# Where the two state-free matmuls stand in a ConvLSTM step

## The reference

```
def step(carry, xr):
    h, c = carry
    inp = jnp.concatenate([xr, h], axis=1)
    gates = lax.conv_general_dilated(inp, w_mid, (1,), 'SAME', ...) + b[None, :, None]
    i, f, g, o = jnp.split(gates, 4, axis=1)
    c2 = jax.nn.sigmoid(f) * c + jax.nn.sigmoid(i) * jnp.tanh(g)
    h2 = jax.nn.sigmoid(o) * jnp.tanh(c2)
    return ((h2, c2), h2)
```

## Time and profile before

| | |
|---|---|
| median of 3 runs | 1986.39 us (1983.12 to 1989.28) |
| the profiled execution's own time | 1985.13 us |
| its span | 1983.2 us |
| mean granted TensorE clock | 0.93 |
| PE busy | 1589.4 us (80%) in 13002 matmuls |
| DVE, ACT, POOL busy | 1475.4, 1172.0, 642.3 us |
| the two scans | about 275 to 798 us and 916 to 1443 us |

### The profile page before, as it was taken

One profiled execution on the slowest core, in us unless ns is written; L12 is line 12 of the kernel. 1 busy time (PEld: TensorE's weight loads), 2 busy tenths in 40 slices (PEclk: granted clock), 3 DMA queues, 4 the chain that ended last, 5 costly groups with the idle time before them and its releaser, 6 DMA issues. The chain is left out here.

```text
span 1983.2 us, 41167 instructions
## 1 busy us (share of the span) xinstructions
PE 1589.4 (80%) x13002; PEld 935.5 (47%) x13002; DVE 1475.4 (74%) x2699; ACT 1172.0 (59%) x2257; POOL 642.3 (32%) x577
## 2 busy tenths in 40 slices
PE   8979248888888888704888888888860899999997
PEld 6535125555555555203555555555520344445444
DVE  4539978888888888646888888888856766666666
ACT  1116128888888888543888888888853344444431
POOL 2010035555555555203555555555500000000000
PEclk9989669999999999857999999999985799999999
DMA  3769366666666666666666666667576011011100
GB/s 108 254 196 211 97 137 108 108 106 107 107 107 107 107 106 91 113 147 131 106 107 107 107 107 107 107 108 108 81 121 164 14 34 34 21 31 35 35 19 25
DMA packets 132266, 199.40 MB, mean 101 GB/s; under 512 B 28528, under 2 KB 47824, under 8 KB 131920
## 3 DMA queue, kind: packets, MB, share of 16 engines
q1 hardware_dynamic: 132176, 198.08, 53.7%
HBM read 73.72 MB, written 37.75 MB: 56 GB/s over the span
## 5 line engine op out<-in xcount | busy, mean ns | idle before, releaser
L720 PE MATMUL gates_l<-xh_l,w_l 128*112 128x512 f32 x3072 | 801.5, 409 | 122.3 <-ACT xh_l L757 122.1
L720 PEld LDWEIGHTS gates_l<-xh_l,w_l 128*112 128x112 f32 x3072 | 500.3, 175 | 422.8 <-issue 288.8
L684 POOL TENSOR_TENSOR xh_l<-hs,xh_l 48x512 fp32r<-48x512 f32 x252 | 300.5, 1192 | 442.0 <-ACT xh_l L757 442.0
L693 POOL TENSOR_TENSOR xh_l<-xf_l,xs_l 48x512 fp32r<-48x512 f32 x256 | 311.7, 1217 | 33.2 <-DVE xs_l L809 32.8
L720 PE MATMUL gates_l<-xc_l,w_l 128*112 128x512 f32 x512 | 164.6, 403 | 135.1 <-DVE begun_l L829 135.1
L853 DVE TENSOR_TENSOR hs<-gate_o_l,tanh_c_l 48x256 f32 (+1 forms) x512 | 193.3, 416 | 73.9 <-ACT tanh_c_l L786 70.1
L1292 PE MATMUL b_dw<-b_hid,b_diag 32*32 32x512 f32 x6840 | 235.3, 602 | 0.0
L786 ACT ACTIVATE tanh_c_l<-cell_l 48x256 f32<-48x256 f32 x512 | 158.1, 342 | 91.4 <-DVE cell_l L844 91.4
L776 ACT ACTIVATE gate_if_l<-gates_l 112x512 f32<-112x512 f32 x256 | 151.4, 591 | 99.8 <-PE gates_l L720 96.6
L844 DVE TENSOR_TENSOR cell_l<-keep_l,gates_l 48x512 f32<-48x512 f32 x256 | 178.5, 697 | 26.7
L840 DVE TENSOR_TENSOR gates_l<-gate_if_l,gates_l 48x512 f32<-48x512 f32 x256 | 178.4, 697 | 21.5
(11 more groups left out here) (150 smaller groups left out, 1436.3 us busy)
## 6 DMA issues: line engine op xcount, KB each, us to landing
xc_l<-xs_l SPq DMA_DIRECT2D x512, 99.0 KB, 3.0
xh_l<-xs_l SPq DMA_DIRECT2D x512, 66.0 KB, 2.4
xf_l<-rows SPq DMA_DIRECT2D x256, 96.0 KB, 2.2
hs<-rows SPq DMA_DIRECT2D x32, 384.0 KB, 10.3
rows<-hs SPq DMA_DIRECT2D x32, 384.0 KB, 5.1
xr<-in_x_rows SPq DMA_DIRECT2D x24, 256.0 KB, 2.7
xc<-in_x_cols SPq DMA_DIRECT2D x24, 256.0 KB, 3.0
mixed<-stage SPq DMA_DIRECT2D x24, 256.0 KB, 3.0
```

Of the source, the lines that this page charges most:

```text
L684: pool.tensor_tensor(inner(xh[n:n + C, d, 1 - s, LO, :]), whole, inner(xh[n:n + C, d, 1 - s, HI, :]).bitcast(F32), ALU.subtract).then_inc( ...
L693: pool.tensor_tensor(inner(xh[f:f + C, d, s, HI, :]), wide(xf[f:f + C, s, :]), inner(x_rows(s, slice(f, f + C))).bitcast(F32), ALU.subtrac ...
L720: return nc.tensor.matmul(ps[d][m][0:K, :], w[:, d, q, m, :], padded(tile)[:, :, lo:lo + W], start=first, stop=last)
```

## The change

In TensorE's block the xc pair moves from ahead of the HI group to between the HI group and the LO group. The waits that stood ahead of it stay where they are, so all the waits of xc and HI now come ahead of HI. The first matmul into each bank is now tap 0 of the HI group, and it carries the start flag. Nothing else is changed: the same 14 matmuls, the same semaphores and counts, the same queues elsewhere.

```
                             pe.wait_ge(sig_if[d], 2 * k + (s + 1))
                             pe.wait_ge(sig_o[d], 2 * k + (s + 1))
                             pe.wait_ge(cells[d], 2 * k + (s + 1))
-                            for m in range(2):
-                                chunk(m, 0, xc[:, d, s, :], 1, first=True)
                             pe.wait_ge(x_lo[d], 2 * k + (s + 1))
                             pe.wait_ge(h_hi[d][0], 2 * k + (s + 1))
                             pe.wait_ge(h_hi[d][1], 2 * k + (s + 1))
                             for m in range(2):
                                 for t in range(3):
-                                    chunk(m, 1 + t, xh[:, d, s, HI, :], t)
+                                    chunk(m, 1 + t, xh[:, d, s, HI, :], t, first=(t == 0))
+                            for m in range(2):
+                                chunk(m, 0, xc[:, d, s, :], 1)
                             pe.wait_ge(h_copy[d], 2 * k + (s + 1))
                             pe.wait_ge(h_lo[d], 2 * k + (s + 1))
                             for m in range(2):
```

## The result

The changed kernel takes 2003.43 us (median of 4 runs, 2002.6 to 2005.4), and the one before 1987.84 us (4 runs, 1983.12 to 1991.44). The ratio is 1.0085, with a 95% interval of 1.0066 to 1.0104: 0.85% slower, 17 us. The forecast was 2008 us, 1995 to 2024. The profiled execution took 2003.45 us with a span of 2000.6 us, 17.4 us more than before.

A forecast was written before the change was run, and what follows sets the result against it. A ScalarE-VectorE loop without matmuls was taken to bound the kernel; the moved pair makes line 757 0.18 us late a period, times 126 is 22.7 us, on 1985.13 or the median 1986.39 us: 2008 us, range 1995 to 2024.

The forecast's parts named there:

- What bounds: A loop through ScalarE and VectorE (lines 757, tanh, new cell, 853) with no matmul sets the 8.15 us period.
- Removal ahead of HI gives nothing: TensorE idles ahead of HI (0.67 and 0.32 us), waiting for the state, so HI starts no earlier without the pair.
- The pair's cost, 0.48 us: Between HI and LO the two xc matmuls delay LO by two spacings of 0.24 us; bounds 0.39 to 0.64 us.
- The signal: Time from a matmul's end to ScalarE's start of line 776, taken as 0.04 us; 0.12 us as the dear bound.
- the sum of 22.7 us: Line 757 of d = 0 comes 0.18 us late each period, over 126 periods.
- The slack of 0.30 us in the short half: From line 757 of d = 1 to that of d = 0: 0.17 us at line 776 plus 0.13 us behind it.
- The long half's cover of 0.15 us: From line 757 of d = 0 to that of d = 1, VectorE's line 809 hides the pair by 0.15 us.
- Refills by SyncE and line 693 cost nothing: Refills of xh and xc and GpSimd's line 693 come later but serve a step over 8 us away; nothing taken.
- Clock: TensorE's clock, at 1.00 with 88.33 us busy of 100, was assumed to stay there at 86.4 us busy.
- Hidden: Rival: the pair costs less than the 0.30 us before anything moves, for instance 0.26 us; about 1986 us; chance 0.13.
- Faster: Rival: the pair's writes delay ScalarE's tanh behind line 757; moving them gives 0.12 us a period, about 1971 us; chance 0.04.
- Dearer: Rival: TensorE stops at the wait behind the pair, costing more than its spacings; about 2030 us or more; chance 0.11.

The follow-up runs named there:

- 693 later: Kernel before plus one more GpSimd wait, so line 693 of d = 1 starts later and GpSimd idles during line 809's copy; ratio to before 0.9971.
- 693 later, moved: Kernel before with that extra wait on line 693 of d = 1, plus the xc pair between HI and LO in both directions; 2050.76 us, ratio 1.0344.
- late-low pair: Kernel before plus a GpSimd operation delaying the state's low part, without and with the xc pair between HI and LO; 2105.45 and 2106.58 us.
- late-low kernel: Kernel before plus one GpSimd operation of line 684's size ahead of line 684, delaying the state's low part; 2105.45 us, ratio 1.0624.

## Why the prediction was right, point by point

*What bounds.* Right in the main, and shown: the loop through ScalarE and VectorE with no matmul in it. A wait for TensorE in d = 0's steps costs nothing, and one in d = 1's costs all. One link is named wrong. The prediction goes from line 757 (1003.00) to the tanh (1003.32), which ends at 1003.89, and says that the other half is the same. In this half, line 840 starts 0.12 us behind that end, but 0.03 us behind line 837's, which came through VectorE's own queue behind line 858:

```profile
1003.29 0.69 DVE L837 TENSOR_TENSOR keep_l<-gate_if_l,cell_l 48x512 f32<-48x512 f32 x1
...
1004.01 0.69 DVE L840 TENSOR_TENSOR gates_l<-gate_if_l,gates_l 48x512 f32<-48x512 f32 x1
```

So the path that opens the short half is line 853, line 858, line 837, and ScalarE has some 0.1 us to spare there. "693 later" shows it: a copy of line 860 that is 0.11 us longer makes this half 0.11 us longer, though the tanh keeps its place. The pair's cost was not touched by this, since line 757 comes late at the start of the long half, where line 840 (1007.97) does follow the tanh's end (1007.37 + 0.57 = 1007.94).

*Removal ahead of HI gives nothing.* Right: HI starts 0.55 us behind line 757's start before and after (1003.00 and 1003.55; 1004.42 and 1004.97).

*The pair's cost, 0.48 us.* A little too high; this is the term that was mis-sized. From HI's start to the end of the third LO matmul it was 1005.97 - 1003.55 = 2.42 us and is 1007.82 - 1004.97 = 2.85 us, so the pair cost 0.43 us net (0.41 us on average over 400 to 600 us). Its two spacings are 0.24 and 0.23 us, 0.47 us together, so some 0.04 us of what stood between HI and LO before is gone. The low part of the state arrived just as HI ended, and with the pair in between it is long there when LO comes. The long half bears this out: there line 684 ended on average 0.07 us earlier against HI, LO followed HI at the plain 0.24 us, and the pair moved the third LO matmul by 0.48 us. I had put such a hole at a loop's turn only, though my own sum for the short half (3.14 us against 3.04 + 0.06) left these 0.04 us over. The signal was 0.03 us, not 0.04. Together these are 0.06 us a period: 0.18 - 0.06 = 0.12 us, which is what the two periods shown differ by (4.05 and 3.93), and 0.06 x 126 = 7.6 us of the sum of 22.7 us. The mean over the scans was 0.130 us.

*The slack of 0.30 us in the short half.* Right: one matmul of 0.24 us fits, two don't, and four cost the full spacing.

*The long half's cover of 0.15 us.* Right in size: with the move in d = 0 alone the half doesn't grow, and its path through line 776 measures 4.08 us against 4.23 us. Right also that the cover is line 809's: without it the half drops by 0.155 us, to where the path through line 776 stands. Not borne out is the sentence that without this cover the pair would cost in the long half what it costs in the short one: without line 809 it cost 0.005 us there, because the long half was still 0.13 us longer than the short one. What the prediction didn't see is why line 809 takes 0.72 us. The cover is GpSimd's instruction, not the copy's work.

*Refills by SyncE and line 693 cost nothing.* Right here. In "693 later, moved" a late signal of TensorE, there bank 0's, decides where a GpSimd instruction starts, and the move costs 74 us; so it holds only while nothing near the path waits on that signal.

*Clock.* Right, 1.00 before and after.

*Rivals.* "Hidden" fell with the result, and its 0.26 us for the pair with the measured 0.43 us. "Faster" fell: the tanh still comes 0.44 us behind the line 757 of 1008.47, at 1008.91, though the next pair no longer runs beside it and LO ends 0.05 us into it (1006.94 + 1.58 = 1008.52). "Dearer" fell: no stop at the wait behind the pair.

## What to carry to other kernels

State-free work is free ahead of a wait at which the engine idles anyway, and behind it costs what exceeds the slack up to the consumer's next instruction. Read that slack from both waits in the consumer's queue, the instruction that takes the result and the one behind it, in each phase of the loop apart. It is free behind the wait only if the next operand is late, as the late-low pair shows. And a new wait of a consumer in the list of waits is no cost by itself: in d = 0 it replaced a wait that was there.

## What the runs showed of the hardware that I had not expected

- A VectorE copy from fp32 to fp32r that starts while a GpSimd tensor operation runs ends only after it: half a row took 0.62 and 0.76 us on average and a whole row 0.72 us, and a whole row took 0.43 us with GpSimd idle. A copy of 48x256, 0.29 us alone, took 0.87 us. GpSimd can be held too: in the late-low kernel its line 698, recorded from 561.15 us while VectorE's copy ran until 561.47 us, took 1.37 us in place of 1.20 us. VectorE's two-input operation of line 844 (one input in PSUM) took 0.70 us with GpSimd's line 693 beside it and, in "693 later", 0.70 us with GpSimd idle.
- TensorE's spacing for fp32r matmuls of 512 columns with a weight load each was 0.24 us in every kernel at a granted clock of 1.00, also with fourteen or sixteen in a row.
